# Gather and scatter groups that wait for a landing only when their slot is needed again, late chunks taken whole, and one block of dense work in a later loop

## The reference

```python
h = jnp.maximum(_layernorm(x, axis=-1), 0.0)
x = x + _L0_gnn_ref(h, edge_index, W3, b3, W4, b4)           # two SGConv layers (gather, segment sum, matmul)
h = jnp.maximum(_layernorm(x, axis=-1), 0.0)
x = x + _L1_gnn_ref(h, edge_index, edge_attr_64, W, b, eps)  # relu(x[src] + edge_attr), segment sum, matmul
h = jnp.maximum(_layernorm(x, axis=-1), 0.0)
x = x + _L2_gnn_ref(h, attn_w, temp, src, dst)               # 8 steps of edge-softmax attention
h = jnp.maximum(_layernorm(x, axis=-1), 0.0)
x = x + _L3_gnn_ref(h, src, dst)                             # 10 steps of normalised propagation
```

## Time and profile before

| | |
|---|---|
| time, median of 3 runs | 8733.76 us (8731.84 to 8740.58) |
| time of the profiled execution | 8729.41 us |
| its span, first to last instruction | 8727.7 us |
| POOL busy | 5692.2 us (65%) |
| DVE busy | 5433.3 us (62%) |
| PE busy | 1657.1 us (19%) |
| ACT busy | 822.7 us (9%) |
| moved by DMA | 660.41 MB, mean 76 GB/s |

### The profile page before, as it was taken

How to read it: one execution, slowest core, us unless ns; L and a number is a source line. 1 busy time by engine, 2 the same in 40 slices (tenths; PEclk the granted TensorE clock), 3 DMA queues, 4 the chain that set the end, 5 groups by cost and what they waited for, 6 DMA issues and landing times.

```text
span 8727.7 us, 64259 instructions
## 1 busy us (share of the span) xinstructions
PE 1657.1 (19%) x7784; PEld 1200.8 (14%) x7784; DVE 5433.3 (62%) x18685; ACT 822.7 (9%) x2015; POOL 5692.2 (65%) x5754
## 2 busy tenths in 40 slices
PE   5744434220234105520022101000000000000000
PEld 1233323110223103410012101000000000000000
DVE  6678868656798623347878788656566564444520
ACT  0011112100112421100000000000006000000000
POOL 5767767554776667757677574476551667777777
PEclk8755555555555555555555555555555555555555
DMA  7034424210245323753434312243323122433310
GB/s 250 2 93 97 98 63 105 57 46 2 60 103 126 93 70 93 219 158 95 132 104 112 81 46 66 55 45 43 37 34 83 46 60 44 42 42 41 36 25 19
DMA packets 1197896, 660.41 MB, mean 76 GB/s; under 512 B 1057323, under 2 KB 1070560, under 8 KB 1195204
## 3 DMA queue, kind: packets, MB, share of 16 engines
q10 hardware_dynamic: 880608, 373.78, 15.6%
q0 software_dynamic: 174720, 155.54, 12.1%
q1 hardware_dynamic: 142436, 129.95, 4.9%
HBM read 236.69 MB, written 425.58 MB: 76 GB/s over the span
## 4 chain that ended last, share of the span: by engine, by line
POOL 42%; DVE 23%; issue 22%; DMA 9%; ACT 1%; POOLq 1%; DVEq 1%; ACTq 0%; SPq 0%; PE 0%
POOL G L574 17%; POOL look L574 7%; DVE G L2132 5%; POOL X L574 4%; POOL pair L574 4%; POOL seatmap L578 4%; POOL out L578 4%; DVE G L2122 1%; DMA G<-tab,idxs 1%; POOL wide_block L574 1%; DMA X<-in_x,dst_gat 1%; DVE xm L1626 1%; DVE st L1596 1%; DMA look<-flagtab,idxs 1%; DVE G L2445 1%
## 5 line engine op out<-in xcount | busy, mean ns | idle before, releaser
L574 POOL DMA_INDIRECT G<-tab,idxs x1260 | 1314.2, 1043 | 452.3 <-issue 357.9
L574 POOL DMA_INDIRECT look<-flagtab,idxs x588 | 624.4, 1062 | 206.3 <-issue 170.1
L574 POOL DMA_INDIRECT G<-alt_e,idxs x420 | 439.3, 1046 | 150.9 <-issue 119.9
L574 POOL DMA_INDIRECT X<-in_x,dst_gat x392 | 415.2, 1059 | 184.7 <-issue 123.5
L574 POOL DMA_INDIRECT pair<-lookup,idxs x392 | 420.6, 1073 | 140.4 <-issue 116.4
L578 POOL DMA_INDIRECT seatmap<-vals,idxs x392 | 408.4, 1042 | 140.8 <-issue 116.6
L1287 PE MATMUL TR<-w4T,shared 128*128 128x64 f32 x2356 | 465.5, 388 | 156.2 <-ACT shared L1007 156.2
L574 POOL DMA_INDIRECT G<-alt_d,idxs x392 | 402.7, 1027 | 138.8 <-issue 115.1
L1596 DVE BATCH_NORM_STATS2 st<-xin 128x6 f32<-128x64 f32 x3136 | 419.2, 211 | 117.3 <-issue 68.9
L1287 PEld LDWEIGHTS TR<-w4T,shared 128*128 128x128 f32 x2356 | 452.0, 298 | 249.7 <-issue 249.7
L1304 PE MATMUL HP<-ident,tcar 128*64 128x128 f32 (+1 forms) x21 | 8.7, 415 | 2323.8 <-DVEq L1521 2313.2
(11 more groups left out here) (528 smaller groups left out, 7621.0 us busy)
## 6 DMA issues: line engine op xcount, KB each, us to landing
tab<-wide_block ACTq DMA_DIRECT2D x294, 448.0 KB, 3.8
tab<-rowsB ACTq DMA_DIRECT2D x98, 448.0 KB, 3.8
xin<-tab SPq DMA_DIRECT2D x84, 448.0 KB
raw<-G ACTq DMA_DIRECT2D x84, 448.0 KB
xin<-in_x SPq DMA_DIRECT2D x56, 448.0 KB, 5.1
tab<-wide_block ACTq DMA_DIRECT2D x2, 12544.0 KB, 55.3
out<-shared ACTq DMA_DIRECT2D x56, 448.0 KB, 5.5
staged<-wide_block SPq DMA_DIRECT2D x20, 1120.0 KB, 5.2
```

Source lines behind the costliest of these rows:

```text
L574: pool.indirect_dma_start(to, None, table, bass.IndirectOffsetOnAxis(ap=index, axis=0), bounds_check=bound, oob_is_err=False).then_inc(s, 16)
```

## The change

- Seat scatter, lookup and looks: the two first groups are issued ahead of the loop. In the loop POOL waits, for each slot in turn, until the group issued one turn earlier from this slot has landed, takes its result where there is one (`keep`, `take`), and issues the slot's next group. The last two are taken behind the loop. In the looks a register `at_turn` counts the turns, since the number of groups is only known then.
- The gather of x is as it was.
- Late chunks of the first attention step: the slot 1 chunk is taken whole, as that of slot 0, with one exponential, and its wide operations in the three `PARTS`.
- `DURING[0]` is 10 where it was 11, so that one dense pair more, 8, runs beside the gather of x.

```diff
-        DURING = [11, 4, 2, 1, 0, 2]
+        DURING = [10, 4, 2, 1, 0, 2]
...
-            with pool.Fori(0, NCH // 2) as i:
+            def seat(c, s):
+                pool.tensor_copy(idxs[:, s, :], cols(end0, c))
+                pool.tensor_copy(vals[:, s, :], cols(place0, c)).then_inc(pool_step, 1)
...
+                for j in range(CH):
+                    scatter(seatmap, idxs[:, s, j:j + 1], vals[:, s, j:j + 1], seated[s])
+            def seat_landed(s):
+                pool.wait_ge(seated[s], r_seat[s].more(16 * CH))
+                pool.sem_inc(pool_waited, 1)
+            for s in (0, 1):
+                seat(s, s)
+            with pool.Fori(1, NCH // 2) as i:
                 for s in (0, 1):
...
-                for s in (0, 1):
-                    pool.wait_ge(seated[s], r_seat[s].more(16 * CH))
-                    pool.sem_inc(pool_waited, 1)
+                    seat_landed(s)
+                    seat(2 * i + s, s)
+            for s in (0, 1):
+                seat_landed(s)
...
+            for s in (0, 1):
+                find(s, s)
+            with pool.Fori(1, NCH // 2) as i:
+                for s in (0, 1):
+                    keep(2 * i + (s - 2), s)
+                    find(2 * i + s, s)
+            for s in (0, 1):
+                keep(NCH - 2 + s, s)
...
+                for s in (0, 1):
+                    look_at(s, s)
+                pool.reg_mov(at_turn, 0)
+                with pool.Fori(1, NCH // 2) as i:
                     with pool.If(i * (2 * CH) < short_cols):
                         for s in (0, 1):
+                            take(2 * i + (s - 2), s)
+                            look_at(2 * i + s, s)
+                        pool.reg_add(at_turn, at_turn, 1)
+                last_turn = pool.snap(at_turn, min_val=0, max_val=NCH // 2 - 1)
+                for s in (0, 1):
+                    take(last_turn * 2 + s, s)
...
+            def staged_chunk(c, s, last=False):
+                exps()
+                if not last:
+                    turn_copy(CH, TR_OF[1 - s])
+                store_raw(seats(alt_d, 0, c), s, AW)
...
-                    for j0, j1 in PIECES[s]:
+                    for j0, j1 in PIECES[0] if late else PIECES[s]:
```

More of the change, by code:

```diff
@@ L605, in _ @@
             last_row(seatmap)
[L606 to L617 removed]
+            def seat(c, s):
+                pool.tensor_copy(idxs[:, s, :], cols(end0, c))
+                pool.tensor_copy(vals[:, s, :], cols(place0, c)).then_inc(pool_step, 1)
+                pool.wait_ge(pool_step, r_step.more(1))
+                pool.sem_inc(pool_waited, 1)
+                last_row(seatmap)
+                for j in range(CH):
+                    scatter(seatmap, idxs[:, s, j:j + 1], vals[:, s, j:j + 1], seated[s])
+            def seat_landed(s):
+                pool.wait_ge(seated[s], r_seat[s].more(16 * CH))
+                pool.sem_inc(pool_waited, 1)
+            for s in (0, 1):
+                seat(s, s)
+            with pool.Fori(1, NCH // 2) as i:
+                for s in (0, 1):
+                    seat_landed(s)
+                    seat(2 * i + s, s)
+            for s in (0, 1):
+                seat_landed(s)
             pool.dma_start(smap[0:NHI, :], seatmap.rearrange("(p j) f -> p (j f)", p=NHI)).then_inc(map_loaded, 16)
@@ L628, in _, with find, keep @@
             last_row(lookup)
-            with pool.Fori(0, NCH // 2) as i:
-                for s in (0, 1):
[L631 to L642, removed]
+            def find(c, s):
+                pool.tensor_copy(idxs[:, s, :], cols(src0, c)).then_inc(pool_step, 1)
+                pool.wait_ge(pool_step, r_step.more(1))
+                pool.sem_inc(pool_waited, 1)
+                last_row(lookup)
+                for j in range(CH):
+                    gather(pair[:, s, j, :], lookup, idxs[:, s, j:j + 1], found_some[s])
+            def keep(c, s):
+                pool.wait_ge(found_some[s], r_fs2[s].more(16 * CH))
+                pool.sem_inc(pool_waited, 1)
+                pool.tensor_copy(found[:, ds(c * CH, CH), :], pair[:, s, :, :]).then_inc(pool_step, 1)
+                pool.wait_ge(pool_step, r_step.more(1))
+                pool.sem_inc(pool_waited, 1)
+            for s in (0, 1):
+                find(s, s)
+            with pool.Fori(1, NCH // 2) as i:
+                for s in (0, 1):
+                    keep(2 * i + (s - 2), s)
+                    find(2 * i + s, s)
+            for s in (0, 1):
+                keep(NCH - 2 + s, s)
             pool.sem_inc(found_all, 1)
@@ L649, in _, with look_at, take @@
             r_cr = Reached(pool, "pool_cr")
+            at_turn = pool.alloc_register("pool_turn")
+            def look_at(c, s):
+                pool.tensor_copy(idxs[:, s, :], cols(listI, c)).then_inc(pool_step, 1)
+                pool.wait_ge(pool_step, r_step.more(1))
+                pool.sem_inc(pool_waited, 1)
+                last_row(flagtab)
+                for j in range(CH):
+                    gather(look[:, s, j:j + 1], flagtab, idxs[:, s, j:j + 1], looked[s])
+            def take(c, s):
+                pool.wait_ge(looked[s], r_lk[s].more(16 * CH))
+                pool.sem_inc(pool_waited, 1)
+                pool.tensor_copy(cols(got, c), look[:, s, :]).then_inc(pool_step, 1)
+                pool.wait_ge(pool_step, r_step.more(1))
+                pool.sem_inc(pool_waited, 1)
             with pool.Fori(0, LEVELS + 1):
@@ L1199, in _, with raw_chunk @@
             root(2)
-            def raw_chunk(table, c, s, then=None):
+            def raw_chunk(table, c, s):
                 for _ in PIECES[s]:
                     exps()
-                if then is not None:
-                    turn_copy(CH, TR_OF[then])
                 store_raw(seats(table, 0, c), s, AW)
+            def staged_chunk(c, s, last=False):
[3 more added lines that the diff above has]
+                store_raw(seats(alt_d, 0, c), s, AW)
             def step_end():
@@ L2395, in attention_chunk @@
                             dve.wait_ge(gathered_rest, r_rest.more(16 * (j1 - j0)))
-                        attention_piece(c, s, j0, j1, PARTS if s == 0 else [(j0, j1)], late)
+                        attention_piece(c, s, j0, j1, PARTS if s == 0 or late else [(j0, j1)], late)
                 def attention_piece(c, s, j0, j1, parts, late):
```

24 lines of the change are left out of this document (5 added, 19 removed).

## The result

The changed kernel takes 8591.56 us (median of 4 runs, 8577.54 to 8598.17); the kernel before, run beside it, took 8734.91 us. The ratio is 0.9833, 95% interval 0.9816 to 0.985. The gain is 143 us where 94 were forecast, and 8591.56 lies outside the range of 8615 to 8675. POOL is GpSimd and DVE is VectorE. A name with a q behind it (POOLq) is the engine's sequencer, the part that goes through the instruction stream: it issues work to the engine, waits on semaphores, and does the register work and the branches itself.

The account below looks back on a forecast made before the run. POOL's chain of indirect DMA groups was taken to set most of the time, with DVE waiting for it. Terms 40 + 18 + 26 - 5 + 15 = 94 us gave 8639 us as a median, range 8615 to 8675.

Parts of the forecast that it names:

- the looks' term: Five rounds of looks: 33.1 us of landing waits go, less dearer handoffs, 21.2 to 28.7 us gained, 26 taken.
- Handoffs: Lookup and looks: a copy out of `pair` ending before the next index copy costs 0.51 us, in twice as many places.
- the lookup: Lookup on POOL: 24.5 us of landing waits go, 6.6 us more for handoffs, 17.9 us gained.
- Seats: Seat scatter on POOL: all 13 landing waits at the turns' ends removed, 40.2 us gained.
- The moved pair: Last dense loop: 54.3 of DVE's 95.0 us of cover at the front rows used, 41 stay; 5 us lost on POOL.
- the pair's company: Gather of x: 61.4 us more beside dense work slows POOL's groups by 1.6 us each, 5 us lost, bounds 0 and 10.
- The rule cited from the Trainium skill: Gather of x: a GpSimd DMA takes about 3100 ns, not 620, beside a VectorE copy; the loss would be 97 us.
- Late chunks: First attention step: 5 chunks taken whole at 13.37 us instead of 16.41, 15 us gained, bounds 5 and 18.
- arrears: Rival, POOL's gathers: landings fall behind without pauses, the 84 us are lost, gain 10 us, 8724; chance 0.06.
- DVE over POOL: Rival, first sweep: DVE becomes the later one, 20 us land on the path, 74 us gained, 8660; chance 0.06.
- loads met: Rival, late chunks: load and dots take 2.8 us longer, DVE waits, 5 us saved there, 8649; chance 0.06.
- pays microseconds a turn for its place: Rival, POOL's rebuilt loops: instructions fetched at every turn, 290 us at 6.9 us a turn, 8929, slower; chance 0.04.

Follow-up runs that it names:

- Experiments 1 and 2: Kernel before with the looks alone changed: ratio 0.992, with pauses kept 0.9944; 14 more tested failing turns a round: kernel before 1.0043, changed kernel 0.9838.
- looks with pauses of experiment 1: Kernel before with the looks alone changed, but each turn waits for both slots, copies both, then issues both groups: 8683.79 us, ratio 0.9944.
- added turns with a single addition: Kernel before with 14 more turns behind each round's loop of looks, whose test is really made and always fails: 8765.18 us, ratio 1.0043.
- kernels with two semaphores: Changed kernel, gather of x waiting for the group before: 8544.91 us; also with a dense pair moved to the first round of looks: 8533.58, repeated 8532.3.

## Why the prediction was wrong

- **The step that failed** is the looks' term: "Five waits, one a round, stay at 1.3 us: 33.1 us go", less the handoffs, "I take 26", and "In the looks no round can give more than about 12 us". What the term names is right as far as it goes, and it was mis-sized because a second part was put at nothing: it counted only waits between instructions that have busy time. The loop's turns that only fail their test stand in none of POOL's waits, yet held `look_done`, the signal for which DVE waits, back by 31.1 us in all. They now run behind queued gathers. The looks gave 63 us: 31 of landing waits, 30 of turns, 3 of handoffs where a loss of 7 was taken (they sum to 64.8; the 63.2 are measured). The five rounds gave 16.9, 14.0, 10.4, 8.0 and 12.8 us, so three of them are over the 12 us that were to be the most; the fourth, with one turn entered and no wait between turns to save, gave 8.0, all of it from its 13 failing turns. The prediction had seen that turn and test "now stand behind gathers that POOL is still busy with", and used it only to choose between 21 and 29. Experiments 1 and 2 show both halves: the turns cost their full time when POOL has nothing queued, and nothing when queued work covers them.
- **Handoffs** were priced at 0.51 us from a row in which each held the loop's turn too. A copy that follows the other without it has 0.27 (7.0 us in 26, in the waits of the changed kernel; 4.3 in 16 in the looks with pauses of experiment 1). That is why the lookup gave 24.5 us and not 18. Its waits also scatter: the lookup takes 609.9 to 619.4 us in seven kernels that wait for each turn's own landings, and 585.2 to 591.2 in the ten that don't, 29 us by the means.
- **Seats**: 43.6 against 40; right.
- **The moved pair**: right that DVE has to be kept ahead: with eleven pairs it comes 14 us late at the lookup's end, and the kernel is 11 to 16 us slower. POOL comes to the front rows 33.6 us behind DVE's last result (3089.30 less 3055.71) where 41 were reckoned, and DVE's wait there is 35.8 us where about 45 were. The 5 us for the pair's company in the gather of x don't show between the two profiles (602.0 and 601.5), but the 14 profiles with the pauses scatter from 596.3 to 617.2. Nine of them have 7 pairs beside the gather and take 601.7 us on average, five have 8 and take 609.6: 8 us, twice the standard error of such a difference. Without the pauses the gather took 548.4 us with the eighth pair and 544.6 and 543.8 without: 4 us. So the term was about right, and that it doesn't show in the table is scatter. The rule cited from the Trainium skill ("SBUF — State Buffer", "A bandwidth-pool intuition that's wrong (but worth ruling out)") is borne out by no row here: a gather of x takes 1058 ns on average in the changed kernel, and the longest of the 392 takes 1709.
- **Late chunks**: 13.36 us a chunk was forecast and is there. 15 us in all were forecast; one pair of profiles shows 14.1, the two groups of kernels 16.6. Only the first late chunk waits for PE, 1.96 us, as it did before (1.95).
- **The rivals**: no arrears (the landing waits that are left are 1.4 to 2.2 us long), DVE over POOL nowhere, loads met nowhere, and no loop of POOL pays microseconds a turn for its place. That tenths of a microsecond a turn change between builds is told below.

## What to carry to other kernels

Ask of every pause at a loop's end what the sequencer does in it, and list register and branch instructions by their line: a loop with a fixed number of turns that skips most of them has a price, and it is paid in full exactly where the engine has nothing left to do. When a wait is put one group later, count as saved not only the wait but all that the sequencer does behind it, up to the work that is queued. And see to the other engine's work first. Two gains here ran into its cover, the time by which DVE still had to wait for POOL: 48.6 us at the lookup's end, where eleven dense pairs were one too many, and 35.8 us at the front rows. There one dense pair, moved from beside the gather of x into the first round of looks, decided whether the front rows came 38 or 52 us earlier.

## What the hardware showed that was not expected

- POOL's sequencer is far ahead of its indirect DMAs: it had issued the last gather of a round about 12 us, some nine gathers, before POOL was through with it (12.3 us in the first round of the changed kernel).
- The same failing turn costs 0.61 us in one build and 0.45 us in another whose code differs only ahead of the loop; of a turn, its addition and branch alone cost 0.21 us. In both builds a turn is the same four instructions of the sequencer, an addition, a branch, register work and the test; behind each of the two branches the next instruction starts some 0.25 us after the branch did in the one build, and some 0.17 in the other. The length of the body that is skipped doesn't decide it: the loop of the looks, with its 28 gathers, costs 0.45 us a turn in the kernel with the lookup alone, as much as the added turns with a single addition (0.46). What decides stays open.
- The kernels that wait for each landing of the gather of x scatter more. The changed kernel's runs lie 20.6 us apart, and those of the ten other such kernels with four or five runs 7.0 to 24.3; those of the kernels with two semaphores 5.6, 5.6 and 4.6 (the last two both with the moved pair). Among the profiles with the waits the gather of x takes 596 to 617 us. That it is what makes the times scatter is likely and not shown, and why a landing takes longer in one execution than in another wasn't tried.
